# Attention row sums from the weighting exponentials, one-term maxima, and normalisation on another engine

## The chip, the cores and the metric

The kernel runs on one core of one Trainium2 chip. The metric is device microseconds of one launch. The median of three runs of the kernel before is 1118.05 us (1117.07 to 1121.98). The profile is of one more execution, which took 1115.44 us.

## The reference

The input x is 4 x 1024 x 512 in float32. Three layers follow one another, each on a layer-normed x, each added to x:

```
x = x + 0.5 * ffn(layernorm(x))        # ternary weights 512x512, plus bias
x = x + attn(layernorm(x))
x = x + 0.5 * ffn(layernorm(x))

attn: kqv = x @ Wqkv + bqkv            # 16 heads of 32
      scores = k . q / sqrt(32), masked to a triangle
      attn = softmax(scores, axis=2); out = attn^T-weighted v; out @ Wo + bo
```

## The kernel before

**Tiles and stages.** A batch has 1024 rows, 8 tiles of 128. The 16 heads are taken in 4 groups of 4; the four heads of a group lie in four bands of 32 partitions. Queries are taken in two chunks of 512 columns (c = 0, 1), keys in blocks of 128. A *step* is one key block of one chunk, or two narrow ones. Chunk 0 has 3 steps, chunk 1 has 7, so a group has 10 steps (`STEPS`), and 4 batches of 4 groups have 160.

**Precision.** Most products are made of three terms: each operand is split into a high part (`HI`, ScalarE writes it from PSUM) and a low part (`LO`, VectorE subtracts), and HI·HI, LO·HI and HI·LO are summed. The fp32 product of `values` is one of full width.

**The order of work** is written out by hand in tables of rows, one row per step (`GROUP0_ROWS` and so on). All five engines walk the same list `SLOTS`. In a slot TensorE does the scores of step n (`scores`, L1266, then the row of maxima by `mneg`, L1274), the weighting by `values` of step n−1 (L1294), and then the slot's *uses*: `A` (product for the maxima, L1232), `M`, `N` (transposes of maxima and inverses, L1242, L1247), `C` (spreading of the inverses over the heads, L1251), `T1` to `T3` (transposes of normalised tiles `hn`, L1184), `P` (queries and keys), `V` (values), `O` (output product; all L1173) and `F1`, `F2` (feed-forward, L1195). `A` runs about nine steps ahead of the scores that use its maxima.

**Softmax.** For each `A` VectorE adds the mask and takes the maximum of each row (`maximum`, L909), and writes the masked scores out. ScalarE takes exponentials of these with the accumulator on (`block_sums`, L1073), only to get the row sums. The sums of two key chunks are combined (`combine`) and inverted on VectorE (`inverse`, L937), turned into rows by `N`, sent by SP to `rall`, and spread by `C`. The exponentials that weight the values are a second set, on the turned scores (`exponentials`, L1099); GpSimd sets those above the diagonal to zero (L808), and `values` waits for that. At the end of a chunk ScalarE takes the sum out of PSUM (`evacuate`, L1063) and VectorE multiplies by the inverse (`scaled`, L945).

**The rest.** VectorE takes the statistics of a tile (L859, L861), GpSimd makes `rstd` of them (L756, L759), VectorE writes `hn` (`normal`, L878), GpSimd adds the bias (L769) and the low part of `o` (L776). PSUM has 8 banks: one collects `values`, seven go round in the order of use (`Banks`), four at once for a step's scores and for an `A`. `prob` has two buffers of four heads by 512.

## Time and profile before

| | before |
|---|---|
| median of three runs | 1118.05 us |
| the profiled execution | 1115.44 us |
| its span, first to last instruction | 1113.7 us |
| TensorE busy | 1067.9 us, 96% |
| weight loads of TensorE | 691.1 us, 62% |
| VectorE busy | 738.9 us, 66% |
| ScalarE busy | 921.7 us, 83% |
| GpSimd busy | 344.0 us, 31% |
| mean granted TensorE clock | 0.983 of full |
| DMA, mean | 70 GB/s |

An engine's busy time is the union of its instructions, and a matmul's record is longer than its pitch, since matmuls are pipelined. For what an instruction costs TensorE, the pieces of the chain are better.

### The profile page before, as it was taken

The page shows a single profiled execution, that of the slowest core. Times are in us where ns is not written, and L with a number is a line of the kernel's source. Part 1 is how long each engine was busy: PE and PEld are TensorE (multiplying, and loading weights), DVE is VectorE, ACT ScalarE, POOL GpSimd, SP SyncE. Part 2 cuts the span into 40 slices and gives each one's busy share as a digit, 9 for nine tenths or more (in the row PEclk, how much of TensorE's full clock was granted, in tenths as well). Part 3 has the DMA queues.
Part 4 walks back from the last instruction along what each step waited for, and adds up shares of the span by engine and source line. Part 5 has one row for each costly group of instructions (what it writes and reads, how often), then busy time and mean ns, then how long its engine had stood idle before and what let it go on. Part 6 is the DMA issues. An engine that isn't in the chain of part 4 may idle for free.

```text
span 1113.7 us, 26124 instructions
## 1 busy us (share of the span) xinstructions
PE 1067.9 (96%) x9472; PEld 691.1 (62%) x9472; DVE 738.9 (66%) x2306; ACT 921.7 (83%) x2577; POOL 344.0 (31%) x471
## 2 busy tenths in 40 slices
PE   5799999999999999999999999999999999999896
PEld 3576656565666565665666666675666666665465
DVE  6866577787535767789644766789744667765344
ACT  2269998999989989889988988878988998999641
POOL 3841232233001313345201322435401322311343
PEclk8898999999999999999999999999999999998999
DMA  6463211021004110421112211421112212000121
GB/s 207 153 217 125 97 50 40 3 78 50 24 19 154 32 59 31 158 73 43 38 41 87 77 59 50 144 78 40 51 40 86 69 40 69 21 12 13 60 66 38
DMA packets 42015, 77.71 MB, mean 70 GB/s; under 512 B 5536, under 2 KB 11680, under 8 KB 41888
## 3 DMA queue, kind: packets, MB, share of 16 engines
q1 hardware_dynamic: 41888, 76.04, 20.5%
q8 instruction: 76, 1.25, 0.5%
q14 instruction: 51, 0.42, 0.1%
HBM read 49.81 MB, written 25.17 MB: 67 GB/s over the span
## 4 chain that ended last, share of the span: by engine, by line
PE 76%; ACT 11%; DVE 6%; issue 2%; POOL 2%; DMA 1%; SPq 0%; DVEq 0%; ACTq 0%; POOLq 0%
PE bank L1173 31%; PE bank L1294 10%; PE bank L1232 10%; PE bank L1266 10%; PE bank L1195 7%; ACT masked_scores L1073 6%; ACT prob L1099 4%; PE bank L1184 3%; PE bank L1274 3%; DVE masked_scores L909 2%; DVE st L859 1%; DMA xt<-in_L_attn_x_dram 1%; DVE hn L878 1%; POOL xt L769 1%; PE bank L1251 1%
## 5 line engine op out<-in xcount | busy, mean ns | idle before, releaser
L909 DVE CUSTOM_DVE_ANT_0 masked_scores<-bank,mask 128x512 f32<-128x512 f32 (+3 forms) x768 | 379.6, 554 | 221.3 <-PE bank L1232 220.2
L1073 ACT ACTIVATE masked_scores<-masked_scores,mst 128x512 f32<-128x512 f32 (+3 forms) x768 | 467.7, 620 | 2.9 <-DVE mst L909 2.9
L1099 ACT ACTIVATE prob<-bank 128x512 f32<-128x512 f32 (+1 forms) x640 | 302.0, 559 | 58.5 <-PE bank L1274 57.4
L1173 PE MATMUL bank<-hT,wqk 128*128 128x512 f32 x768 | 190.9, 397 | 0.0
L808 POOL TENSOR_SCALAR_AFFINE_SELECT prob<-prob 128x512 f32<-128x512 f32 (+1 forms) x96 | 78.6, 819 | 346.5 <-ACT prob L1099 345.8
L1266 PE MATMUL bank<-qT,kT 32*128 32x512 f32 (+2 forms) x2304 | 169.6, 378 | 4.5 <-DVE kT L886 1.6
L1232 PEld LDWEIGHTS bank<-kT,qT 32*128 32x128 f32 x2304 | 94.4, 185 | 115.6 <-issue 52.8
L1232 PE MATMUL bank<-kT,qT 32*128 32x512 f32 (+2 forms) x2304 | 161.2, 377 | 3.4 <-ACT prob L1099 2.6
L1173 PEld LDWEIGHTS bank<-hT,wqk 128*128 128x128 f32 x768 | 140.4, 188 | 37.9 <-ACT prob L1099 8.2
L1073 ACT ACTIVATION_READ_ACCUMULATOR masked_scores<-masked_scores,mst 128x1 f32 x768 | 156.4, 204 | 0.0
L1266 PEld LDWEIGHTS bank<-qT,kT 32*128 32x128 f32 x2304 | 97.7, 185 | 70.4 <-issue 48.4
L1195 PE MATMUL bank<-wfT,hts 128*128 128x512 f32 x512 | 138.3, 414 | 1.5 <-DVE hts L884 1.5
L1294 PE MATMUL bank<-prob,v 128*32 128x512 f32 (+3 forms) x1344 | 138.7, 500 | 0.0
L1195 PEld LDWEIGHTS bank<-wfT,hts 128*128 128x128 f32 x512 | 94.4, 194 | 24.5 <-ACT prob L1099 2.6
L769 POOL TENSOR_TENSOR xt<-xt,hb 128x512 f32<-128x512 f32 x64 | 82.3, 1286 | 77.0 <-DVE hn L878 77.0
L1173 PE MATMUL bank<-wvo,hts 128*128 128x512 f32 x384 | 97.2, 403 | 5.0 <-POOL hts L776 5.0
L1173 PE MATMUL bank<-wvo,hT 128*128 128x512 f32 x384 | 96.1, 402 | 1.2 <-DVE qT L886 1.2
L1173 PEld LDWEIGHTS bank<-wvo,hts 128*128 128x128 f32 x384 | 70.7, 190 | 24.4 <-ACT prob L1099 6.0
L1173 PEld LDWEIGHTS bank<-wvo,hT 128*128 128x128 f32 x384 | 71.3, 191 | 19.5 <-ACT prob L1099 2.7
L1184 PE MATMUL bank<-ident,hn 128*128 128x128 f32 x384 | 59.7, 284 | 13.5 <-DVE hn L878 13.5
L1274 PE MATMUL bank<-mneg,onesr 2*128 2x512 f32 (+2 forms) x768 | 69.9, 350 | 2.1 <-DMA mneg<-mrow 2.1
L859 DVE BATCH_NORM_STATS2 st<-xt 128x6 f32<-128x512 f32 x96 | 65.9, 686 | 5.2 <-DMA xt<-in_L_attn_x_dram 3.2
(87 smaller groups left out, 971.7 us busy)
## 6 DMA issues: line engine op xcount, KB each, us to landing
wqk<-weight_scratch SPq DMA_DIRECT2D x30, 512.0 KB, 3.4
wvo<-weight_scratch SPq DMA_DIRECT2D x20, 512.0 KB, 6.0
xt<-in_L_attn_x_dram SPq DMA_DIRECT2D x32, 256.0 KB, 4.2
residual_scratch<-xt SPq DMA_DIRECT2D x32, 256.0 KB, 2.0
xt<-residual_scratch SPq DMA_DIRECT2D x32, 256.0 KB, 3.1
out_dram<-xt SPq DMA_DIRECT2D x32, 256.0 KB, 2.0
o<-in_L_attn_Wqkv_dram SPq DMA_DIRECT2D x12, 256.0 KB, 4.7
weight_scratch<-o SPq DMA_DIRECT2D x6, 512.0 KB, 3.0
```

Source lines behind the costliest of these rows:

```text
L769: nc.gpsimd.tensor_tensor(to, to, (bo2 if l == 1 else hb)[:, :], ALU.add).then_inc(xb_done[l], 1)
L808: nc.gpsimd.affine_select(out=part, in_=part, compare_op=ALU.is_ge, fill=0.0, base=0, pattern=[[0, 4], [0, m], [1, P]], channel_multiplier ...
L909: nc.vector.tensor_tensor_reduce(masked_scores[:, h, at:at + n], psum(u, h)[:, at:at + n], mask[:, off:off + n], -SCALE, BIG, ALU.add, ALU ...
L1073: nc.scalar.activation(of, of, ACT.Exp, bias=mst[:, c + kc, to:to + 1], scale=-1.0, accum_out=ssum[:, c + kc, to:to + 1]).then_inc(a_free, 1)
L1099: nc.scalar.activation(prob[:, at % 2, h, off:CW], psum(("S", b, n), h)[:, off:CW], ACT.Exp, scale=SCALE)\
L1173: m = nc.tensor.matmul(psum(u), left(x, k), right(y, k), start=(n == 0), stop=(n == len(terms) - 1))
L1184: m = nc.tensor.transpose(psum(u)[:, P * k:P * k + P], hn[:, TURN[u] % 2, P * k:P * k + P], ident[:, :])
L1195: m = nc.tensor.matmul(psum(u), h[:, part, k, :], wfT[:, k, :], start=(k == 0 and part == HI), stop=(k == KC - 1 and part == LO))
L1232: m = nc.tensor.matmul(psum(u, h)[:, at:at + n], query_piece(b, g, c)[row, x, P * r:P * r + P], kT[g % 2][row, y, CW * kc:CW * kc + n], st ...
L1266: nc.tensor.matmul(psum(u, h)[:, at:at + CW - off], kT[g % 2][row, x, P * kb:P * kb + P], query_piece(b, g, c)[row, y, off:CW], start=(ter ...
L1274: m = nc.tensor.matmul(psum(u, h)[:, at:at + CW - off], onesr[row, :], mneg[row, c, off:CW], start=False, stop=(kb == keys[-1]))
L1294: m = nc.tensor.matmul(accv[HD * h:HD * h + HD, off:CW], v_of(b, g, kb, h), prob[:, at % 2, h, of:of + CW - off], start=(kb == 0), stop=(k ...
```

## The change

The block exponentials of `masked_scores` are no longer made. The sums now come from the exponentials that weight the values: `prob` gets a third buffer, the first step of a chunk stays in its buffer as the running total, and the exponentials of each later step are added to it, heads 0 and 1 by VectorE, heads 2 and 3 by GpSimd (10 additions per group and engine). A new use `E` multiplies the total by a matrix of ones, which gives each head's sums on its 32 partitions. ScalarE copies them out, a DMA lays them out over all 128 partitions, VectorE inverts them there and splits the inverse into two parts, and a DMA brings it back as rows for `C`. In the last group (`direct`) there is no such trip: `over_sums` inverts and multiplies in four pieces.

`A` is made of one term instead of three. VectorE takes the maximum of blocks off the diagonal with a plain reduction; those on the diagonal keep the masking instruction. The row of maxima is one row per head instead of a high and a low one. ScalarE instead of VectorE normalises (`hn`), with three instructions. The tables of rows are new: `E` stands in a chunk's second slot and belongs to the chunk before, `N` two slots later and `C` four; in the middle batches parts of the feed-forward move from group 2 to group 1. `evacuate` is no longer bound to `C`: it follows the exponentials of the next chunk's first step.

```diff
+def direct(b, g):
+
+    return (b, g) == (B - 1, GROUPS - 1)
...
-    "C T3.3 P | A | X3.6",
-    "N M F2.3 P | A | X3.7",
-    "P | A",
-    "C O.4 | A",
-    "O.5 | A",
-    "N T3.4 O.6 | A",
-    "M F2.4 | A",
-    "T3.5 O.7 | A | X1.0",
-    "T3.6 F2.5 | A | LV X1.1",
-    "T3.7 F2.6 P | A | X1.2",
+    "T3.3 P | A | X3.6",
+    "E M F2.3 | A | X3.7",
+    "T1.0 O.4 | A",
+    "N F1.0 P | A | X1.1",
+    "E O.5 | A",
+    "C O.6 | A",
+    "N M T3.4 P | A | X1.2",
+    "F2.4 | A",
+    "T3.5 O.7 | A",
+    "C T1.1 F2.5 P | A | LV X1.3",
...
+NPROB = 3
+
+
+def homes():
+
+
+    free, at, total = [0] * NPROB, [], None
+    for n in range(B * NSTEP):
+        first = step_of(n % STEPS)[1][0] == 0
+        here = min(range(NPROB), key=lambda m: free[m])
+        assert free[here] <= n
+        if first and total is not None:
+            free[total] = n + 2
+        if first:
+            total = here
+        free[here] = B * NSTEP + NPROB if first else n + 2
+        at.append(here)
+    return at
+
+
+HOME = homes()
...
+        def additions(n, heads):
+
+            c, keys = step_of(n % STEPS)
+            for j, kb in enumerate(keys):
+                off = first_query(c, kb)
+                yield (prob[:, HOME[chunk_first(n)], heads, off:CW],
+                       prob[:, HOME[n], heads, off - HALF * j:CW - HALF * j])
...
-                sp.wait_ge(ring_free, freed(u))
-                for part in (HI, LO):
-                    sp.dma_start(mneg[part:P:HD, c, :].bitcast(F32), mrow[:, c, part, :].bitcast(F32))\
-                        .then_inc(mrow_in[c], 16)
+                sp.wait_ge(row_done, ROWS[u] + 1)
+                sp.dma_start(mneg[0:P:HD, c, :].bitcast(F32), mrow[:, c, :].bitcast(F32)).then_inc(mrow_in[c], 16)
+
+            def sums_to_columns(u):
+
+                sp.wait_ge(sums_out, ended(u) + 1)
+                if ended(u):
+                    sp.wait_ge(inverse_done, 3 * ended(u) - 2)
+                sp.dma_start(scol[:, :], sums[0:P:HD, :].rearrange("h (j x) -> h j x", x=4 * QPC)).then_inc(sums_in, 16)
 
             def inverse_rows(u):
                 _, b, g, c = u
-                sp.wait_ge(ring_free, freed(u))
+                sp.wait_ge(inverse_done, 3 * ended(u) + 3)
                 if ended(u):
                     sp.wait_ge(ring_full, full(("C", b, g, c - 1) if c else ("C", *before(b, g), 1)))
                 for part in (HI, LO):
-                    sp.dma_start(rall[4 * part:4 * part + 4, :].bitcast(F32), rrow[:, part, :].bitcast(F32))\
-                        .then_inc(rall_in, 16)
+                    sp.dma_start(rall[4 * part:4 * part + 4, :].bitcast(F32).rearrange("h (j x) -> h j x", x=4 * QPC),
+                                 rsplit[:, part, :].bitcast(F32)).then_inc(rall_in, 16)
...
+            def add(n):
+
+                f = chunk_first(n)
+                if n == f:
+                    return
+                if diagonal(n % STEPS):
+                    pool.wait_ge(masked, diagonals(n))
+                else:
+                    pool.wait_ge(s_exp, 4 * n + 4)
+                pool.wait_ge(value_done, f + 1)
+                for j, (to, of) in enumerate(additions(n, slice(2, 4))):
+                    if ADDED[n - 1]:
+                        pool.wait_ge(added_pool, ADDED[n - 1] + j)
+                    nc.gpsimd.tensor_tensor(to, to, of, ALU.add).then_inc(added_pool, 1)
...
+                if s.step is not None and step(s.b, s.step):
+                    add(step(s.b, s.step) - 1)
+                elif (s.b, s.row) == (B, 0):
+                    add(B * NSTEP - 1)
...
-                    if EARLIER[u] is not None:
-                        dve.wait_ge(a_free, block_at(EARLIER[u], h))
+                    written = COUNTED[u] + max(0, h - 1) * len(u[5])
+                    if kc == c and written:
+                        dve.wait_ge(a_max, written)
                     for j, r, at, n, off in block_tiles(u):
-                        to = 4 * h + r
-                        nc.vector.tensor_tensor_reduce(masked_scores[:, h, at:at + n], psum(u, h)[:, at:at + n],
-                                                       mask[:, off:off + n], -SCALE, BIG, ALU.add, ALU.min,
-                                                       mst[:, c + kc, to:to + 1]).then_inc(a_max, 1)
+                        of, to = psum(u, h)[:, at:at + n], mst[:, c + kc, 4 * h + r:4 * h + r + 1]
+                        if kc < c:
+                            i = nc.vector.tensor_reduce(to, of, AX, ALU.max)
+                        else:
+                            i = nc.vector.tensor_tensor_reduce(masked_scores[:, h % 2, at:at + n], of, mask[:, off:off + n], 1.0, -BIG,
+                                                               ALU.add, ALU.max, to)
+                        i.then_inc(a_max, 1)
                 if u == maxima(b, g, 1)[-1]:
                     dve.wait_ge(a_max, block_at(u))
-                    nc.vector.tensor_tensor(mcol[:, :], mst[:, 1, :], mst[:, 2, :], ALU.min).then_inc(mcol_done, 1)
-                    dve.wait_ge(mcol_done, group(b, g))
-                    for n in range(2):
-                        i = nc.vector.tensor_tensor(msh[:, n, :], mst[:, 1 + n, :], mcol[:, :], ALU.subtract)
-                    i.then_inc(shift_done, 1)
-
-            def combine(u):
-
-                at = group(u[1], u[2])
-                dve.wait_ge(shift_exp, at)
-                nc.vector.tensor_tensor(msh[:, :, :], msh[:, :, :], ssum[:, 1:3, :], ALU.mult).then_inc(inverse_done, 1)
-                dve.wait_ge(inverse_done, 4 * at - 2)
-                nc.vector.tensor_tensor(msh[:, 0, :], msh[:, 0, :], msh[:, 1, :], ALU.add).then_inc(inverse_done, 1)
+                    nc.vector.tensor_tensor(mcol[:, :], mst[:, 1, :], mst[:, 2, :], ALU.max).then_inc(mcol_done, 1)
+
+            def add(n):
+
+                f = chunk_first(n)
+                if n == f:
+                    return
+                if diagonal(n % STEPS):
+                    dve.wait_ge(masked, diagonals(n))
+                else:
+                    dve.wait_ge(s_exp, 4 * n + 2)
+                dve.wait_ge(value_done, f + 1)
+                for j, (to, of) in enumerate(additions(n, slice(0, 2))):
+                    if ADDED[n - 1]:
+                        dve.wait_ge(added, ADDED[n - 1] + j)
+                    nc.vector.tensor_tensor(to, to, of, ALU.add).then_inc(added, 1)
...
+                at = 3 * ended(u)
+                dve.wait_ge(sums_in, 16 * ended(u) + 16)
+                nc.vector.reciprocal(rcol[:, :], scol[:, :]).then_inc(inverse_done, 1)
+                if ended(u):
+                    dve.wait_ge(rall_in, 32 * ended(u))
+                dve.wait_ge(inverse_done, at + 1)
+                nc.vector.tensor_copy(rsplit[:, HI, :], rcol[:, :]).then_inc(inverse_done, 1)
+                dve.wait_ge(inverse_done, at + 2)
+                nc.vector.tensor_tensor(rsplit[:, LO, :], rcol[:, :], rsplit[:, HI, :].bitcast(F32), ALU.subtract)\
+                    .then_inc(inverse_done, 1)
...
+            def over_sums(u):
 
                 _, b, g, c = u
+                dve.wait_ge(ring_full, full(u))
                 dve.wait_ge(accv_free, ended(u) + 1)
-                dve.wait_ge(ring_full, full(u))
-                of = chunk(b, CHUNKS * g + c)
-                nc.vector.tensor_tensor(of, psum(u), of, ALU.mult).then_inc(ring_free, 1)
+                for r in range(QPC):
+                    at = slice(P * r, P * r + P)
+                    of = chunk(b, CHUNKS * g + c)[:, at]
+                    if c:
+                        dve.wait_ge(piece_done, r + 1)
+                    nc.vector.reciprocal(sums[:, at], psum(u)[:, at]).then_inc(inverse_done, 1)
+                    dve.wait_ge(inverse_done, 3 * ended(("E", b, g, 0)) + QPC * c + r + 1)
+                    nc.vector.tensor_tensor(of, of, sums[:, at], ALU.mult).then_inc(piece_done, 1)
...
-            def block_sums(u, heads):
-
-                _, b, g, c, kc, _ = u
-                for h in heads:
-                    for j, r, at, n, _ in block_tiles(u):
-                        to = 4 * h + r
-                        act.wait_ge(a_max, block_at(u, h, j))
-                        of = masked_scores[:, h, at:at + n]
-                        nc.scalar.activation(of, of, ACT.Exp, bias=mst[:, c + kc, to:to + 1], scale=-1.0,
-                                             accum_out=ssum[:, c + kc, to:to + 1]).then_inc(a_free, 1)
-                if u == maxima(b, g, 1)[-1] and 3 in heads:
-                    act.wait_ge(shift_done, group(b, g))
-                    nc.scalar.activation(msh[:, :, :], msh[:, :, :], ACT.Exp, scale=-1.0).then_inc(shift_exp, 1)
...
+            def sums_away(u):
+
+                act.wait_ge(ring_full, full(u))
+                if ended(u):
+                    act.wait_ge(sums_in, 16 * ended(u))
+                nc.scalar.activation(sums[:, :], psum(u), ACT.Identity).then_inc(sums_out, 1)
+
+            def normal(u):
+                kind, b, t = u
+                l = int(kind[1]) - 1
+                k = TURN[u]
+                if k >= 2:
+                    act.wait_ge(ring_full, full(TRANSPOSED[k - 2]))
+                if l == 0:
+                    act.wait_ge(*loaded(xw(kind, b, t)))
+                act.wait_ge(rs_done[l], tile(b, t))
+                nc.scalar.activation(nmean[:, l, t:t + 1], mv[:, l, t, 0:1], ACT.Identity, scale=-1.0).then_inc(shift_done, 1)
+                act.wait_ge(shift_done, 2 * k + 1)
+                nc.scalar.activation(shift[:, l, t:t + 1], nmean[:, l, t:t + 1], ACT.Identity, scale=rstd[:, l, t:t + 1])                    .then_inc(shift_done, 1)
+                act.wait_ge(shift_done, 2 * k + 2)
+                nc.scalar.activation(hn[:, k % 2, :], x_tile(xw(kind, b, t)), ACT.Identity, bias=shift[:, l, t:t + 1],
+                                     scale=rstd[:, l, t:t + 1]).then_inc(hn_done, 1)
...
+                held = [m for m in range(at) if HOME[m] == HOME[at]][-1:]
+                for m in held:
+                    if chunk_first(m) == m:
+                        i = m % STEPS
+                        act.wait_ge(ring_full, full(("E", m // NSTEP, m % NSTEP // STEPS, 1 if i else 0)))
+                    else:
+                        act.wait_ge(value_done, m + 1)
+                        act.wait_ge(added, ADDED[m])
+                        act.wait_ge(added_pool, ADDED[m])
                 for h in range(4):
-                    nc.scalar.activation(prob[:, at % 2, h, off:CW], psum(("S", b, n), h)[:, off:CW], ACT.Exp, scale=SCALE)\
+                    nc.scalar.activation(prob[:, HOME[at], h, off:CW], psum(("S", b, n), h)[:, off:CW], ACT.Exp, scale=SCALE)\
...
-                    for term, (x, y) in enumerate(((HI, HI), (LO, HI), (HI, LO))):
-                        for j, r, at, keys, _ in block_tiles(u):
-                            n = max(HALF, keys)
-                            for h in range(4):
-                                if term == 0 and j == 0:
-                                    bank_free(u, h)
-                                row = slice(HD * h, HD * h + HD)
-                                m = nc.tensor.matmul(psum(u, h)[:, at:at + n], query_piece(b, g, c)[row, x, P * r:P * r + P],
-                                                     kT[g % 2][row, y, CW * kc:CW * kc + n], start=(term == 0 and j == 0),
-                                                     stop=(term == 2 and j == len(u[5]) - 1))
+                    for j, r, at, keys, _ in block_tiles(u):
+                        n = max(HALF, keys)
+                        for h in range(4):
+                            if j == 0:
+                                bank_free(u, h)
+                            row = slice(HD * h, HD * h + HD)
+                            m = nc.tensor.matmul(psum(u, h)[:, at:at + n], query_piece(b, g, c)[row, HI, P * r:P * r + P],
+                                                 kT[g % 2][row, HI, CW * kc:CW * kc + n], start=(j == 0),
+                                                 stop=(j == len(u[5]) - 1))
...
+                elif kind == "E":
+                    n = last_step(u)
+                    pe.wait_ge(added, ADDED[n])
+                    pe.wait_ge(added_pool, ADDED[n])
+                    for h in range(4):
+                        m = nc.tensor.matmul(psum(u)[HD * h:HD * h + HD, :], ones[:, 0:HD], prob[:, HOME[chunk_first(n)], h, :],
+                                             start=True, stop=True)
+                    m.then_inc(ring_full, 1)
...
-                        row = slice(HD * h, HD * h + 2)
+                        row = slice(HD * h, HD * h + 1)
```

## Rows read from the trace of the kernel before

**Rows 1.** The page: TensorE's part of the busy line, and the chain by engine.
```profile
PE 1067.9 (96%) x9472; PEld 691.1 (62%) x9472; DVE 738.9 (66%) x2306; ACT 921.7 (83%) x2577; POOL 344.0 (31%) x471
...
PE 76%; ACT 11%; DVE 6%; issue 2%; POOL 2%; DMA 1%; SPq 0%; DVEq 0%; ACTq 0%; POOLq 0%
```

**Rows 2.** Stretches: us from:to, length, then busy us of each engine.
```profile
0.00:103.20 103.20, 80.51 (x440) 58.55 (x442) 74.66 (x183) 50.11 (x132) 52.60 (x75) 0.93 0.54 176
103.20:218.90 115.70, 112.80 (x1056) 69.10 (x1052) 77.58 (x268) 108.77 (x310) 31.41 (x46) 0.97 0.17 57
218.90:276.20 57.30, 55.49 (x549) 33.86 (x542) 44.93 (x143) 55.99 (x158) 21.35 (x24) 1.00 0.19 62
276.20:340.50 64.30, 64.30 (x586) 41.88 (x582) 29.83 (x113) 56.26 (x163) 4.91 (x6) 1.00 0.13 43
340.50:463.50 123.00, 122.97 (x1160) 79.78 (x1158) 86.22 (x276) 110.67 (x311) 38.31 (x47) 1.00 0.24 80
463.50:532.40 68.90, 67.53 (x618) 44.02 (x614) 61.28 (x179) 58.64 (x161) 32.71 (x49) 1.00 0.18 59
532.40:598.30 65.90, 65.87 (x602) 43.14 (x594) 32.48 (x119) 57.35 (x158) 7.86 (x9) 1.00 0.16 54
856.20:975.50 119.30, 119.30 (x1137) 76.58 (x1134) 82.93 (x267) 110.53 (x317) 34.94 (x50) 1.00 0.16 52
975.50:1027.40 51.90, 50.56 (x501) 29.66 (x497) 32.89 (x118) 50.35 (x146) 7.47 (x8) 0.94 0.04 13
1027.40:1113.70 86.30, 72.12 (x515) 47.30 (x507) 35.27 (x72) 35.25 (x85) 32.38 (x46) 0.94 0.16 53
```

**Rows 3.** The chain in order of time, 521 to 534: start, us it takes, what.
```profile
521.06 1.00 PE bank L1294 x8
522.05 1.15 PE bank L1232 x20
523.20 0.59 PE bank L1184 x4
523.79 1.85 PE bank L1195 x8
...
527.57 0.72 PE bank L1232 x10
...
528.89 2.75 PE bank L1173 x12
531.63 0.90 PE bank L1266 x10
532.53 0.24 PE bank L1274 x4
...
533.56 0.90 PE bank L1232 x10
```

**Rows 4.** The page's groups: busy us, mean ns of one, idle time before.
```profile
L1073 ACT ACTIVATE masked_scores<-masked_scores,mst 128x512 f32<-128x512 f32 (+3 forms) x768 | 467.7, 620 | 2.9 <-DVE mst L909 2.9
```

**Rows 5.** Groups by shape: subtractions of two inputs, VectorE and GpSimd.
```profile
L884 DVE TENSOR_TENSOR hts<-bank,hts 128x512 fp32r<-128x512 f32 x64 | 43.6, 681 | 15.5 <-ACT hts L1039 15.5
...
L776 POOL TENSOR_TENSOR hts<-o,hts 128x512 fp32r<-128x512 f32 x8 | 10.3, 1293 | 18.5 <-ACT hts L1092 18.5
...
L776 POOL TENSOR_TENSOR hts<-o,hts 128x128 fp32r<-128x128 f32 x16 | 7.5, 471 | 18.9 <-ACT hts L1092 18.9
...
L884 DVE TENSOR_TENSOR rrow<-bank,rrow 16x128 fp32r<-16x128 f32 x32 | 8.8, 274 | 3.0 <-ACT rrow L1032 3.0
```

**Rows 6.** Timeline of the tail: start, us, engine, instruction [idle before].
```profile
1087.55 1.59 POOL L776 TENSOR_TENSOR hts<-o,hts 128x384 fp32r<-128x384 f32 x2
1087.69 1.14 DVE L878 TENSOR_SCALAR hn<-xt,mv,rstd 128x512 f32<-128x512 f32 x1 [1.03 <-POOL rstd L759]
...
1091.39 0.55 DVE L878 TENSOR_SCALAR hn<-xt,mv,rstd 128x512 f32<-128x512 f32 x1 [1.02 <-POOL rstd L759]
```

**Rows 7.** Who waited for whom: us in total, times, longest.
```profile
DVE masked_scores L909 <- PE bank L1232: 220.2, 133, 6.0
```

More of the change, by code:

```diff
@@ L238 @@
     "T3.5 O.7",
[L239 to L241 removed]
+    "F2.4",
+    "T3.6 F2.5",
+    "T3.7 F2.6",
     "F2.7",
@@ L278, in __init__ @@
         self.b, self.step, self.row = b, step, row
-        self.whole, self.blocks, self.loads, weights = rows
+        whole, self.blocks, self.loads, weights = rows
+        self.whole = [u for u in whole if u[0] != "N"]
+        self.inverses = [u for u in whole if u[0] == "N"]
         self.weights = [n for _, n in weights]
     def uses(self):
-        return self.blocks + self.whole
+        sums = [u for u in self.whole if u[0] == "E"]
+        return sums + self.blocks + [u for u in self.whole if u[0] != "E"]
 def plan():
@@ L336 @@
 assert len(USES) == len(set(USES))
-SPLIT = {u: n for n, u in enumerate([u for s in SLOTS for kinds in ("M N", "T1 T2 T3", "P") for u in s.uses()
+SPLIT = {u: n for n, u in enumerate([u for s in SLOTS for kinds in ("T1 T2 T3", "P") for u in s.uses()
                                      if u[0] in kinds.split()])}
@@ L389, in use @@
                 self.full[u] = full
-            if u[0] not in ("A", "V") and u not in [TURNED[n] for n in BY_ACT]:
+            if u[0] not in ("A", "V", "M", "E") and u not in [TURNED[n] for n in BY_ACT]:
                 self.freed[u] = freed
@@ L713, in _ @@
                     load(w)
+                for u in s.inverses:
+                    inverse_rows(u)
                 for u in s.uses():
@@ L981, in _ @@
                     first_stats(k)
-                for u in s.uses():
-                    if u[0] == "N":
-                        inverse(u)
-                    elif u[0] == "C" and u[3] == 0:
-                        combine(u)
-                if s.step is None and k > 1:
-                    for u in NORMALISED[k]:
-                        normal(u)
+                for u in s.inverses:
+                    inverse(u)
                 for u in s.uses():
@@ L992, in _ @@
                         use(u)
-                if s.step is not None or k == 1:
-                    for u in NORMALISED[k]:
-                        normal(u)
+                if s.step is not None:
+                    add(step(s.b, s.step))
                 for u in s.uses():
@@ L1105, in _ @@
                     act.wait_ge(s_full, step(b, s.step) + 1)
-                    if step(b, s.step) >= 2:
-                        act.wait_ge(value_done, step(b, s.step) - 1)
                     exponentials(b, s.step)
-                if k and SLOTS[k - 1].blocks:
-                    block_sums(SLOTS[k - 1].blocks[-1], (3,))
+                    g, i = s.step // STEPS, s.step % STEPS
+                    if i == CHUNK_STEPS[0]:
+                        evacuate(b, g, 0)
+                    elif i == 0 and step(b, s.step):
+                        evacuate(*before(b, g), 1)
+                elif (b, s.row) == (B, 0):
+                    evacuate(B - 1, GROUPS - 1, 1)
                 for u in s.uses():
-                    if u[0] in ("M", "N"):
-                        high(u)
-                    elif u[0] == "C":
-                        evacuate(u)
+                    if u[0] == "M":
+                        row(u)
+                    elif u[0] == "E" and not direct(u[1], u[2]):
+                        sums_away(u)
                 for u in s.uses():
@@ L1121, in _ @@
                         high_output(u)
-                for u in s.blocks:
-                    block_sums(u, range(4) if u != s.blocks[-1] else range(3))
+                for u in NORMALISED[k]:
+                    normal(u)
                 for u in s.uses():
@@ L1146, in bank_free @@
                     pe.wait_ge(a_max, block_at(w, n))
+                elif w[0] == "M":
+                    pe.wait_ge(row_done, ROWS[w] + 1)
+                elif w[0] == "E" and direct(w[1], w[2]):
+                    pe.wait_ge(piece_done, QPC * w[3] + QPC)
+                elif w[0] == "E":
+                    pe.wait_ge(sums_out, ended(w) + 1)
                 else:
```

275 lines of the change are left out of this document (132 added, 143 removed).

## The prediction

> **What bounds the kernel now.** I began with the page. TensorE is busy 96% of the span, and the chain that ended last is 76% TensorE, 11% ScalarE and 6% VectorE [rows 1]. ScalarE's part is mostly one line, the exponentials of `masked_scores` (L1073), which exist only to get row sums. Next I cut the span into the head, 15 groups of ten steps and the last group with the tail, and read busy time by stretch [rows 2]. The reader is to see two kinds of stretch. In batch 0, groups 0 to 2 (115.7 us for two, then 57.3), ScalarE is busy 94 to 98% of the time, and TensorE's own work fills only 50 to 52 us a group. I count that work by the pitches of the chain [rows 3]: 0.90 + 0.24 us for a step's scores, 1.00 for its values, 0.90 for a use of `A`, less for narrow ones, which is 29.9 us a group with `C`, `M` and `N`; then 2.75 us for each `P`, `V` or `O`, 1.85 for each `F`, 0.59 for each `T` of the rows. From 276.2 us on the span follows TensorE: groups of 60 to 69 us, in which this count leaves 1 to 4 us open. One group of each middle batch is close on VectorE too: 61.28 us busy of 68.9. GpSimd is busy 5 to 33 us per group and mostly waits. Head and tail are latency: TensorE works 80.5 us of 103.2, and 72.1 of 86.3.
>
> **The change, part by part.** Durations are pitches of the chain where matmuls overlap [rows 3].
>
> *Maxima with one term.* Each of 160 uses of `A` issues a third of its matmuls. A use takes 0.90 us with twelve 512-wide matmuls, 1.15 with twenty-four 256-wide, 0.72 with twelve 384-wide [rows 3]. A group has six, two and two of them: 9.1 us (the last five at the tile sizes of chunk 0 and the diagonal). For four matmuls with 32 or fewer rows, the nearest row is the one that adds `mneg`: 0.24 for four 512-wide ones [rows 3]; eight 256-wide ones are as long. I take 0.24, so 2.4 us a group, and 6.7 us are saved. Between 0.20 and 0.40 a use the saving is 5.1 to 7.1.
>
> *Sums by a ones matmul (`E`), twice a group.* Four fp32 products of 128 rows by 512 columns, of the same form as a step of `values`: 1.00 us for 8 instructions [rows 3], so +2.0 a group. The transpose `N`, smaller than the `T` of 0.59, goes twice, some 0.15 each by its share of columns; `C` and `M` stay. Net for TensorE: −6.7 + 2.0 − 0.3 = −5.0, and as the pieces beside it do not all compress I take −4.7 us a group, 75 us in all.
>
> *ScalarE loses the block exponentials:* 467.7 us [rows 4], and the reads of the accumulator behind them. It gains 96 normalisations: two instructions on 128x1 and one on 128x512, about 1.1 us with the waits on itself, 106 us; 30 copies of sums at 0.6. It lands near 600 us, about 38 us a group. So it bounds no group, and groups 0 to 2 of batch 0 and group 2 of batch 3 are freed to the next limit. Its normalisation waits on GpSimd's `rstd`, and the high parts of `P` and the next step's exponentials are queued behind it. I cost that at nothing, because most rows leave a step or more (5 to 6 us) between statistics and use. If GpSimd runs a step late, it costs 1 to 2 us a row.
>
> *VectorE.* It loses `hn` (96 at 0.5 to 0.55 [rows 6], about 48 us), the low parts of `M` and `N` and the shifts (2 us a group), and gets about 1.2 us of inverses. The off-diagonal maxima become a plain reduction, which I cost as equal, 0.69 us. It gains the additions. There is no addition of this size in the trace. From its own 16x128 and 128x512 subtractions, 274 and 681 ns [rows 5], a column costs 1.06 ns above 138 ns: 1.22, 0.95, 0.68 and 0.41 us for two heads of 512, 384, 256 and 128 columns. A group has 4, 2, 2 and 2 of them: 9.0 us. Net +8.1 − 0.5 for each `hn`: from 77.6 for groups 0 and 1 of batch 0 to about 43 + 48 us, from 44.9 to 48 in group 2, and about 61 in the dense group (61.28 now; it loses 13 `hn` and two tiles move to the group before).
>
> *GpSimd.* Its rows give 471 ns for 128 columns and 1293 for 512 [rows 5], 2.14 ns a column: 2.39, 1.84, 1.29 and 0.74 us, 17.3 us a group, 277 in all. It would be busy 22 to 50 us a group, about 620 us in total. The masking select is queued behind the addition of the step before, and `values` waits for it. But it has about 4 us of room: exponentials end 3.3 us into a step and `values` comes a step and 1.1 us later. Hidden.
>
> *Do the two kinds of addition disturb each other?* This decides the sum. The trace shows one such case: `hn` (SBUF to SBUF) takes 0.55 us by itself and 1.14 when GpSimd's subtraction of two SBUF tiles is running, ending just behind it [rows 6]. Operations of VectorE with one input in PSUM keep their time beside GpSimd. The additions have both inputs in SBUF, and no row shows that form beside GpSimd. Bounds: zero per addition (they pass each other), and a whole GpSimd addition, 1.7 us on average (17.3 / 10), every time. I take half the collisions: GpSimd will be busy about 65% of a group, a hit leaves half an operation, about 0.9 us, so 5.5 us a group. I choose this nearer to the disturbed row because source and destination are alike.
>
> The Trainium skill ("SBUF — State Buffer", section "Who interferes with whom") says that a VectorE instruction with two SBUF inputs contends with a GpSimd instruction that reads SBUF, and that the second to issue blocks until the first has ended. No row here has that form; the rows of `hn` agree with the blocking as such. By that rule the loss is never zero, and the sum is the forecast or the slow rival below, not the fast one.
>
> *New waits.* `E` waits for both engines' additions of the chunk's last step; scores of the next step are queued behind it on TensorE. It stands a step and a half behind them, so nothing. Exponentials wait for the additions of two steps before: nothing unless VectorE is over a step late. On SP the column DMA of the sums waits for ScalarE's copy, with x loads, stores and `mneg` rows queued behind; one `mneg` DMA less and 1 to 2 us of waiting, hidden by a step or more. VectorE's inverse waits for that DMA two steps later, with the maxima queued behind: nothing expected, up to 1 us a time.
>
> **The sum**, against the profiled execution: 1113.7 us of span and 1.7 us around it. A group is the later of TensorE's work and VectorE's with its losses, and 2 us on top where both are near. Head 103.2 → 101 (its last 25 us wait on block exponentials, but weights and loads remain). Batch 0: the first two groups 115.7 together → 51.5 + 55, then 57.3, 64.3 → 55.5, 60. Middle batches: the first two groups 123.0 together → 57 + 60, then 68.9, 65.9 → 67, 63.5, all twice. Batch 3: the first two 119.3 together → 55.5 + 58, then 51.9 → 47 [rows 2]. Last group and tail 86.3 → 85: the sums now come after the last exponentials, and `over_sums` puts a reciprocal between, which eats most of the gain. Total 101 + 222 + 495 + 160.5 + 85 = 1063.5, and with 1.7 us outside, 1065. The median of the runs is 0.2% above the profiled run. I forecast 1064.
>
> **The rivals.**
> *No disturbance, TensorE stays the only bound.* Additions pass or fall where the other engine idles. For it: GpSimd has room, and VectorE waits 220.2 us for the maxima's matmuls [rows 7]. Against it: both additions are released by the same event, and VectorE is near 48 of 50 us even so. Taking the 5.5 us out: batch 0 50, 50, 51, 60; middle 56, 59, 64, 63.5; batch 3 54.5, 57, 44; 1037 in all; with a smaller tail and fewer gaps, 1015.
> *VectorE takes the place of TensorE, slower than now.* Each VectorE addition waits out a whole GpSimd addition, because GpSimd starts at the end of the exponentials or of the mask, about 3.3 to 4.4 us into a step, and VectorE only behind the maxima, about 5 us in. Place: every step but the first of a chunk. Price: 17.3 us a group instead of 5.5. Groups are then 62 to 81 us long, as 48 + 17 + 2 in batch 0 and 61 + 17 + 3 in the dense group: 1150 to 1200 us. It decides from 1.0 us of loss per addition on: each us a group costs about 12 us in all, so 10 us a group gives 1118.
> *The gain is mostly given back.* The same at 0.8 to 0.95 us, or the chains behind GpSimd and the DMA of the sums show as gaps of 2 to 3 us a group: 1085 to 1112.
> That TensorE's work does not fall can hardly be: two thirds of the matmuls of a use go.
>
> **How the numbers follow.** Forecast (1045 to 1085) 0.47; no disturbance (1010 to 1045) 0.28; gain mostly given back 0.14; no net change 0.04; slower 0.07. The range runs from 1015 to 1105. A measurement of this kernel can tell about 0.5% from no change. Faster by more than that: 0.47 + 0.28 + 0.12 = 0.87; within it 0.05; slower 0.08.
>
> **What the profile after would show.** L1232's successor takes a quarter of a us per use and a third of its count. No `masked_scores` on ScalarE, and its share near 57%. `E` at 1.0 us without idle before it. VectorE near 78% and GpSimd near 58% busy. The disturbance would show as a mean of the VectorE additions of 128x1024 well above 1.2 us, or of GpSimd's above 2.4. If it is small, these means stand and the groups of batch 0 come to 50 us. It would prove me wrong if TensorE idled before `E` or before the transposes, which is the path over GpSimd and ScalarE that I cost at nothing, or if plain reductions differ from 0.69 us: 256 of them at 0.1 us are 26 us of VectorE.

## The result and the profile after

| | before | after |
|---|---|---|
| median of the runs | 1118.18 us (4 runs) | 1146.78 us (4 runs, 1143.29 to 1150.02) |
| profiled execution, span | 1115.44, 1113.7 us | 1150.02, 1148.3 us |
| mean granted clock | 0.983 | 0.958 |

The ratio is 1.025, with a 95% interval of 1.021 to 1.029. The change makes the kernel 2.5% slower. I had forecast 1064 us, and a range up to 1105.

The page of the kernel after: busy times, granted clock in 40 slices (tenths), and the chain by engine.

```profile
PE 1070.7 (93%) x8158; PEld 663.4 (58%) x8158; DVE 900.0 (78%) x2058; ACT 608.8 (53%) x1311; POOL 661.4 (58%) x631
...
PEclk8899989797999999989999999999999999998989
...
PE 58%; DVE 21%; POOL 12%; issue 6%; ACT 2%; DMA 1%; SPq 0%; POOLq 0%; DVEq 0%; ACTq 0%
```

ScalarE fell from 921.7 to 608.8 us as expected. But 1536 fewer matmuls of `A` left TensorE's busy time where it was, 1070.7 us, and the chain now runs over VectorE and GpSimd for a third of the span, where it was 8% [rows 1]. The clock is low in more slices.

Stretches of the kernel after, cut at the same steps as in [rows 2]; us from:to, length, busy us of TensorE, weight loads, VectorE, ScalarE, GpSimd, then granted clock, DMA share and GB/s.

```profile
0.00:97.70 97.70, 76.17 (x352) 55.03 (x354) 63.12 (x150) 46.20 (x97) 50.40 (x75) 0.93 0.57 186
97.70:219.20 121.50, 116.09 (x884) 66.84 (x880) 97.36 (x239) 61.70 (x128) 71.32 (x66) 0.89 0.17 54
219.20:285.10 65.90, 61.17 (x467) 34.93 (x461) 56.13 (x124) 41.35 (x91) 41.69 (x35) 0.87 0.17 54
285.10:347.20 62.10, 62.06 (x508) 39.05 (x500) 41.46 (x103) 29.43 (x66) 22.67 (x16) 1.00 0.14 41
347.20:476.20 129.00, 124.11 (x1000) 77.00 (x992) 110.45 (x251) 68.22 (x143) 79.69 (x71) 0.99 0.23 74
476.20:548.80 72.60, 67.05 (x524) 42.15 (x516) 65.16 (x146) 45.28 (x98) 49.99 (x50) 0.95 0.18 59
...
1003.50:1053.40 49.90, 47.68 (x423) 25.89 (x418) 40.88 (x106) 27.12 (x58) 25.66 (x18) 0.95 0.05 13
1053.40:1148.30 94.90, 75.76 (x527) 47.34 (x519) 51.88 (x83) 40.90 (x93) 54.58 (x58) 0.91 0.14 48
```

Against [rows 2]: the head is 5.5 us shorter. Groups 0 and 1 of batch 0 are 121.5 us (115.7 before, 106.5 forecast), group 2 65.9 (57.3, 55.5), the first two of batch 1 129.0 (123.0, 117), the dense group 72.6 (68.9, 67). The last group with the tail lost 8.6 us. The head, the fourth group of batch 0 (62.1 against 64.3) and the third of batch 3 (49.9 against 51.9) gained; the others lost, and no single one explains the result. VectorE is busy 80 to 90% of the groups that lost most, and never all of one.

The additions of the kernel after, by shape: busy us, mean ns of one.

```profile
L852 POOL TENSOR_TENSOR prob<-prob 128x1024 f32<-128x1024 f32 x64 | 174.1, 2720 | 56.0 <-ACT prob L1207 55.3 <-POOL prob L852 0.3
...
L1010 DVE TENSOR_TENSOR prob<-prob 128x1024 f32<-128x1024 f32 x64 | 114.0, 1781 | 1.4 <-POOL prob L895 1.4
...
L1010 DVE TENSOR_TENSOR prob<-prob 128x256 f32<-128x256 f32 x32 | 34.0, 1061 | 1.1
```

I had costed them at 1.22 us, 0.41 us (VectorE) and 2.39 us (GpSimd) by themselves, and 5.5 us a group of blocking on VectorE. All of VectorE's take 224.4 us where 16 groups of 9.0 make 144: 5.0 us a group of blocking. GpSimd's are held up too, by 39 us in all, which I had at nothing. So VectorE's term was sized well; its price was not. The timeline of one step shows how it is paid: start, us, instruction, and idle time before it with what ended it.

```profile
708.78 2.38 POOL L852 TENSOR_TENSOR prob<-prob 128x1024 f32<-128x1024 f32 x1
708.85 3.40 DVE L1010 TENSOR_TENSOR prob<-prob 128x1024 f32<-128x1024 f32 x1
...
711.47 0.50 PE L1348 MATMUL bank<-kT,qT 32*128 32x512 f32 x2
712.17 0.68 DVE L972 TENSOR_TENSOR xt<-bank,xt 128x512 f32<-128x512 f32 x1
...
712.91 0.49 PE L1348 MATMUL bank<-kT,qT 32*128 32x512 f32 x2 [0.94 <-DVE xt L972]
```

GpSimd's addition starts 0.07 us earlier. VectorE's ends 1.1 us behind the end of GpSimd's: 3.40 us for an instruction of 1.22. Behind it in VectorE's queue stands the residual of the last output product, which frees a PSUM bank. `A` of the next slot needs four banks of the ring of seven and gets two: its second pair of matmuls starts 1.44 us after the first, 0.94 us of it idle.

GpSimd's bias instruction (L837, also of two SBUF inputs) blocks in the same way, and VectorE blocks GpSimd:

```profile
126.18 1.29 POOL L837 TENSOR_TENSOR xt<-xt,hb 128x512 f32<-128x512 f32 x1 [1.66 <-ACT hn L1177]
...
126.99 1.57 DVE L1010 TENSOR_TENSOR prob<-prob 128x1024 f32<-128x1024 f32 x1
127.43 3.35 POOL L852 TENSOR_TENSOR prob<-prob 128x1024 f32<-128x1024 f32 x1
```

VectorE's addition ends 1.08 us behind the bias, and GpSimd's then ends 2.2 us behind VectorE's. Over the whole trace, 109 of VectorE's 160 additions lose time in this way, 0.74 us each: 49 us behind GpSimd's additions and 32 us behind its bias and low-part instructions.

### The profile page after: what moved, and what is told of

Same layout as the page of the kernel before. It is cut to its first block, busy times and chain, and to the rows that moved or that the text cites. A ratio compares the mean times of both kernels' runs of the same rounds, so it can differ in the third digit from the quotient of the medians.

```text
span 1148.3 us, 22475 instructions
## 1 busy us (share of the span) xinstructions
PE 1070.7 (93%) x8158; PEld 663.4 (58%) x8158; DVE 900.0 (78%) x2058; ACT 608.8 (53%) x1311; POOL 661.4 (58%) x631
## 3 DMA queue, kind: packets, MB, share of 16 engines
q8 instruction: 66, 1.08, 0.4%
## 4 chain that ended last, share of the span: by engine, by line
PE 58%; DVE 21%; POOL 12%; issue 6%; ACT 2%; DMA 1%; SPq 0%; POOLq 0%; DVEq 0%; ACTq 0%
PE bank L1290 26%; PE bank L1414 8%; PE bank L1386 7%; DVE prob L1010 6%; POOL prob L852 5%; DVE mst L988 5%; PE bank L1348 5%; PE bank L1312 5%; POOL xt L837 3%; PE bank L1369 2%; PE bank L1301 2%; PE bank L1394 2%; DVE st L946 2%; POOL prob L895 2%; DVE masked_scores L990 1%
## 5 line engine op out<-in xcount | busy, mean ns | idle before, releaser
L852 POOL TENSOR_TENSOR prob<-prob 128x1024 f32<-128x1024 f32 (+3 forms) x160 | 315.4, 1971 | 61.6 <-ACT prob L1207 55.3
L990 DVE CUSTOM_DVE_ANT_0 masked_scores<-bank,mask 128x128 f32<-128x128 f32 (+3 forms) x512 | 218.1, 487 | 75.6 <-PE bank L1348 75.5
L1010 DVE TENSOR_TENSOR prob<-prob 128x1024 f32<-128x1024 f32 (+3 forms) x160 | 224.4, 1403 | 16.5 <-POOL prob L895 15.1
L1290 PE MATMUL bank<-hT,wqk 128*128 128x512 f32 x768 | 198.1, 408 | 0.1
L988 DVE TENSOR_REDUCE mst<-bank 128x1 f32<-128x512 f32 x256 | 158.6, 682 | 49.2 <-PE bank L1348 49.1
L1348 PEld LDWEIGHTS bank<-kT,qT 32*128 32x128 f32 x768 | 47.4, 188 | 151.0 <-issue 94.3
L1348 PE MATMUL bank<-kT,qT 32*128 32x512 f32 (+2 forms) x768 | 109.7, 444 | 26.0 <-DVE xt L975 16.7
L837 POOL TENSOR_TENSOR xt<-xt,hb 128x512 f32<-128x512 f32 x64 | 90.9, 1421 | 33.6 <-ACT hn L1177 31.8
L824 POOL TENSOR_SCALAR ve<-mv 128x1 f32<-128x1 f32 x96 | 18.3, 190 | 131.5 <-DVE mv L948 127.1
L1177 ACT ACTIVATE hn<-xt,shift,rstd 128x512 f32<-128x512 f32 x96 | 78.3, 815 | 3.2
```

Source lines behind the costliest of these rows:

```text
L837: nc.gpsimd.tensor_tensor(to, to, (bo2 if l == 1 else hb)[:, :], ALU.add).then_inc(xb_done[l], 1)
L852: nc.gpsimd.tensor_tensor(to, to, of, ALU.add).then_inc(added_pool, 1)
L988: i = nc.vector.tensor_reduce(to, of, AX, ALU.max)
L990: i = nc.vector.tensor_tensor_reduce(masked_scores[:, h % 2, at:at + n], of, mask[:, off:off + n], 1.0, -BIG, ALU.add, ALU.max, to)
L1010: nc.vector.tensor_tensor(to, to, of, ALU.add).then_inc(added, 1)
L1290: m = nc.tensor.matmul(psum(u), left(x, k), right(y, k), start=(n == 0), stop=(n == len(terms) - 1))
```

## The experiments

All are edits of the changed kernel but one. The theory under test: the additions, by the time they take on VectorE with the blocking included, hold up the release of PSUM banks and so TensorE. Where additions are left out, the sums are not those of a whole chunk, and only the time is of use.

**Without any addition.** All calls of both `add` functions go, with the waits on them.

```diff
-                if s.step is not None:
-                    add(step(s.b, s.step))
...
-                    pe.wait_ge(added, ADDED[n])
-                    pe.wait_ge(added_pool, ADDED[n])
```

> The changed kernel with all 320 additions left out (the sums are then those of a chunk's first step), all else kept. Theory: the additions, by their time on VectorE and GpSimd and by blocking each other, are what turned the expected gain into a loss; without them TensorE is the bound and the time is 1035 to 1060 us, with the clock low for at most 50 us. Rival: the loss comes from elsewhere (E at 1.0 us, the trip of the sums, normalisation on ScalarE, the short A); then the time stays above 1100 us.

Measured: 1063.4 us (two runs, 1057.3 and 1069.4), 3 us above the theory's range and far below the rival. The additions cost 83 us (77 to 89 by these two runs); what is left of the change gives 54 us, where the prediction's case without disturbance (1037 us, at best 1015), additions included, had 80 to 100. The chain of this run in order of time (start, us, what) shows why:

```profile
714.99 0.86 PE bank L1359 x8
...
730.11 0.97 PE bank L1376 x11
731.09 0.23 PE bank L1384 x3
731.32 0.99 PE bank L1404 x8
732.31 0.43 PE bank L1340 x2
732.74 0.59 PE bank L1293 x4
```

L1340 is `A` with one term. It takes 0.43 us, although nothing waits here, and not the 0.24 us of the `mneg` rows (L1384 here) that I took from [rows 3]. 160 uses at 0.2 us more are 32 us. (From one matmul's start to the next, `A` takes 70.6 us in this whole trace, 0.44 a use.) `E` (L1359) takes 0.86 us, a little less than my 1.00.

**VectorE's additions alone, GpSimd's alone.** The other engine's calls and the waits on them are left out.

```diff
-                if s.step is not None and step(s.b, s.step):
-                    add(step(s.b, s.step) - 1)
-                elif (s.b, s.row) == (B, 0):
-                    add(B * NSTEP - 1)
```

> GpSimd's 160 additions left out, VectorE's kept where they are. Theory of contention: VectorE's additions fall from a mean of 1403 ns to about 950, as the width alone gives (1.22, 0.95, 0.68, 0.41 us), and the time falls to 1060 to 1085 us. Rival, VectorE's own load and the place of its additions: they keep VectorE late by the same amount, and the time stays at 1115 us or more.

> VectorE's 160 additions left out, GpSimd's kept. Theory that VectorE is what is late (its additions stand in front of the instructions that free PSUM banks): 1045 to 1070 us, nearly as without any. Rival, GpSimd's queue is what is late (mask and rstd behind additions of 2 to 3 us): the time stays above 1100 us.

Measured: 1096.8 us with VectorE's alone, 33 us above none; 1076.9 with GpSimd's alone, 14 above none. The first lies between theory and rival, the second 7 us above the theory's range and far from its rival. Together they should cost 47 us and cost 83. Either more load than VectorE can hide or the meeting of the two makes the missing 36 us; the next run separates these. By shape, first VectorE's alone, then GpSimd's alone:

```profile
L1006 DVE TENSOR_TENSOR prob<-prob 128x1024 f32<-128x1024 f32 x64 | 91.1, 1423 | 0.0
...
L1006 DVE TENSOR_TENSOR prob<-prob 128x256 f32<-128x256 f32 x32 | 17.0, 532 | 1.1
```

```profile
L852 POOL TENSOR_TENSOR prob<-prob 128x1024 f32<-128x1024 f32 x64 | 152.9, 2388 | 56.7 <-ACT prob L1204 55.9 <-POOL prob L852 0.3
```

GpSimd's are within 0.1% of my estimate. VectorE's of 1024 columns are 0.2 us above theirs on average, and all 160 have a mean of 1.07 us, not the 0.95 expected: they meet GpSimd's bias and low-part instructions, which remain and cost them 28 us in this run.

**One SBUF input instead of two on VectorE.** GpSimd's additions stay, and VectorE reads as many elements as an addition has columns, but has no second input, and writes two columns and not the total.

```diff
-                    nc.vector.tensor_tensor(to, to, of, ALU.add).then_inc(added, 1)
+                    nc.vector.tensor_reduce(rsum[:, :], of, AX, ALU.add).then_inc(added, 1)
```

> The changed kernel in which each of VectorE's 160 additions is a sum over the same new exponentials into two scalars (one SBUF input instead of two, about the same length; the totals of heads 0 and 1 are then left out). GpSimd's additions stay. Theory of contention: operations with one SBUF input do not block and are not blocked by GpSimd's; VectorE's take 1.2 us at 1024 columns without spread, GpSimd's go back to 2388 ns from 2720, the time falls from 1147 to about 1105 us, the two halves' costs simply added (33 + 14 us above 1063). Rival, load: the same load on both engines gives the same loss; 1135 us or more.

Measured: 1089.6 us, lower than even the theory's 1105, and 57 us below the changed kernel, with the same count of instructions in the same places. By shape:

```profile
L853 POOL TENSOR_TENSOR prob<-prob 128x1024 f32<-128x1024 f32 x64 | 152.8, 2388 | 56.7 <-ACT prob L1208 55.9 <-POOL prob L853 0.3
...
L1011 DVE TENSOR_REDUCE rsum<-prob 128x2 f32<-128x1024 f32 x64 | 77.4, 1210 | 1.4 <-POOL prob L896 1.4
```

Both engines are back at their undisturbed times. VectorE is busy 815.8 us in this run, 900.0 with the additions: the 84 us of blocking on it, and 39 us on GpSimd (315.4 against 276), turn into 57 us of the span. The form of the operands does it, not the load. That agrees with the Trainium skill ("SBUF — State Buffer", section "Who interferes with whom"): two SBUF inputs contend with GpSimd's reads, a reduction does not. The wide write that the edit also drops is not enough by itself: in the changed kernel the residual additions (L975, one input in PSUM, 512 columns written to SBUF) take 741 ns beside GpSimd's two-input instructions and 744 away from them.

**The addition last in its slot.** VectorE takes the slot's products out of PSUM first.

```diff
-                if s.step is not None:
-                    add(step(s.b, s.step))
                 for u in s.uses():
                     if u in PRODUCTS:
                         use(u)
+                if s.step is not None:
+                    add(step(s.b, s.step))
```

> The whole changed kernel, with VectorE's addition moved behind the instructions of the same slot that take products out of PSUM (P, V, F, O), ahead of the statistics. Theory of place: TensorE's waits at A for banks held by these products (about 50 us in the changed kernel) mostly go, the clock falls less often, and the time is 1100 to 1125 us. Rival: the load of VectorE is what counts and the order does not; within 1% of the changed kernel, 1135 to 1158 us.

Measured: 1133.6 us, 1.1% better than the changed kernel, slower than the theory's 1100 to 1125 and than the kernel before (ratio 1.014, 1.010 to 1.017), and 1.4 us off the rival's range. The place matters a little. Summed from one matmul's start to the next over the whole trace, `A` falls from 119.5 to 73.5 us, near the 70.6 without additions, and the scores with their `mneg` rows rise from 215.9 to 243.5: over half of the wait moves on to the next user of banks. I read this as VectorE being late, whichever release stands last.

**Three terms of `A` put back.**

```diff
-                    for j, r, at, keys, _ in block_tiles(u):
+                    for term, (x, y) in enumerate(((HI, HI), (LO, HI), (HI, LO))):
+                        for j, r, at, keys, _ in block_tiles(u):
```

> The changed kernel with the three terms of A put back. Theory: a good part of what the one-term A saves turns into waits for PSUM banks at A and at the scores, because VectorE sets the pace; the three terms cost only 0 to 30 us more than 1147. Rival, TensorE is the bound: 160 uses at 0.45 to 0.6 us more, 70 to 95 us, 1215 to 1240 us.

Measured: 1183.3 us, 36 us above the changed kernel, between both: my 0 to 30 was a little low. By pitches, 0.90 against 0.43 us, the two terms are worth some 75 us, and only half of that shows. Waits in the changed kernel hide a part. Another part may be clock: its mean is 0.979 here against 0.958, which is 25 us of full clock withheld against 48. No run tells the two apart.

**Other splits of the additions:** one head to VectorE and three to GpSimd, all four to VectorE, all four to GpSimd. The edit of the first:

```diff
-                for j, (to, of) in enumerate(additions(n, slice(0, 2))):
+                for j, (to, of) in enumerate(additions(n, slice(0, 1))):
...
-                for j, (to, of) in enumerate(additions(n, slice(2, 4))):
+                for j, (to, of) in enumerate(additions(n, slice(1, 4))):
```

> The changed kernel with the additions split one head to VectorE and three to GpSimd. GpSimd alone with two heads cost only 14 us, VectorE alone 33. Theory that VectorE's load and place are what costs: its additions are half as long, the time falls to 1110 to 1130 us. Rival, GpSimd: with 0.19 + 2.14 ns a column a step's addition takes 3.5 us, 25 us a group, and blocks VectorE longer each time; 1140 us or more.

> All four heads' additions on VectorE, none on GpSimd; everything else as changed. VectorE then has 266 us of additions (138 ns and 1.06 ns a column, 16.6 us a group) where it now spends 224 with the blocking. Theory that the blocking of the two engines is the larger part: with more addition time on VectorE but hardly any blocking (GpSimd's bias and low-part instructions remain) the time is no higher than 1147, 1115 to 1150 us. Rival, VectorE's time as such sets the pace, whatever fills it: 42 us more of it cost 40 us or more, 1185 us or above.

> All four heads' additions on GpSimd, none on VectorE. GpSimd then has 0.19 us and 2.14 ns a column, 4.6 us for a step of 512, 33 us a group and 525 us in all, which with its 339 us makes 80% of the span. Theory that GpSimd's queue has room as long as VectorE does not contend: 1090 to 1125 us, below 1147. Rival: the mask select and rstd behind 4.6 us additions make TensorE wait at values and at the transposes; 1150 us or more.

Measured: 1184.6, 1169.8 and 1160.2 us. My theory failed all three times. The rival held with one to three (1140 or more) and with all on GpSimd (1150 or more); all on VectorE lies between, 20 us above my range and 15 below the rival. One to three is the worst, where I expected 1110 to 1130. By shape, in that run:

```profile
L852 POOL TENSOR_TENSOR prob<-prob 128x1536 f32<-128x1536 f32 x64 | 232.2, 3628 | 44.1 <-ACT prob L1207 43.3 <-POOL prob L852 0.3
...
L1010 DVE TENSOR_TENSOR prob<-prob 128x512 f32<-128x512 f32 x64 | 112.0, 1750 | 5.8 <-POOL prob L895 5.8
```

An addition of half the size takes VectorE 1.75 us, as long as one of two heads, since it waits out the longer one of GpSimd (0.68 us by itself). With all on VectorE the blocking on it falls to some 28 us (294 us of additions where I had costed 266), but its busy time is 960.7 us, 60 above the changed kernel's. With all on GpSimd, VectorE is busy only 732.7 us; the mask comes late, and TensorE waits for it. Who waited for whom in that run (us in total, times, longest):

```profile
ACT nmean L1171 <- POOL rstd L827: 61.3, 25, 5.1
...
PE bank L1410 <- POOL prob L895: 38.7, 21, 4.0
```

**One-term `A` alone, in the kernel before.** The edit of the change to `A` and nothing else.

> The kernel before with the one-term A alone. If the pitch of a short A is 0.24 us as forecast, TensorE loses 5 to 6.7 us of work a group; in the groups bounded by ScalarE (batch 0 and group 2 of batch 3) nothing comes of it, since ScalarE stays at 55 to 58 us a group and becomes the bound in the others too: 1060 to 1085 us. Rival: the short A is no shorter than 0.45 us with its weight loads, and it waits for banks; then 1090 to 1118 us.

Measured: 1088.2 us, a ratio of 0.975 (0.971 to 0.979) to the kernel before, between the two expectations and nearer to the rival, which had the pitch right. ScalarE's share of the chain is 20% in this run. This part of the change is worth 28 us by itself, and it is the best complete version of this study, 59 us faster than the whole change.

## Why the prediction was wrong

**The cost of the additions by themselves was right** (1.21, 0.95, 0.68 and 0.42 us are the lowest of VectorE's, and 2388, 1840, 1290 and 739 ns are GpSimd's means without VectorE's). **VectorE's blocking was right in kind and size**, 5.0 us a group against 5.5: 68% of the additions are hit, where I took 65%, at 0.74 us each, where I took 0.9. I also named the deciding point: 10 us a group was to give 1118. Half of that gave more.

**The step that failed is "A group is the later of TensorE's work and VectorE's with its losses, and 2 us on top where both are near."** In groups 0 and 1 of batch 0 VectorE is busy 97.4 us, less than the 102 of the forecast (43 + 48, and 11 of losses), and the stretch lasts 121.5, not 106.5. The forecast gave the blocking 27 us of time (1037 to 1064); in the runs the additions with their blocking cost 83, and 57 of these go when VectorE has one input. VectorE does its work in a fixed order, with four PSUM banks for `A` and four for the scores out of seven. The reading that fits the timeline of the step: TensorE waits whenever one release comes late, and does not get the time back. Sorted by VectorE's busy time, seven runs make one row:

| VectorE busy, us | time, us | mean clock | what |
|---|---|---|---|
| 686 | 1063 | 0.974 | no additions |
| 694 | 1077 | 0.984 | GpSimd's alone |
| 816 | 1090 | 0.981 | one input |
| 840 | 1097 | 0.979 | VectorE's alone |
| 884 | 1134 | 0.962 | addition last |
| 900 | 1147 | 0.958 | the change |
| 961 | 1170 | 0.953 | all on VectorE |

From 686 to 840 us, where VectorE is 77% busy, 154 us cost 34; the next 60 us cost 50, and 60 more cost 23. Off the row are the run with three terms, which gives TensorE more work, and the two in which GpSimd is the fullest, 64 and 74% busy (one to three, and all on GpSimd). In the changed kernel both engines are under 80%, and still TensorE does not hide them: that is what the forecast lacked. The table is an ordering by one number, not a proof that only this number counts: a VectorE that is blocked counts as busy, and the clock falls along the same row.

**The pitch of a short `A` was mis-sized.** 0.24 us from the `mneg` rows, which load one or two rows of weights, against 0.43 measured; 32 us in all. My upper bound of 0.40 missed too. It accounts for the run without additions standing at 1063 and not near 1030. From start to start, `A` takes 153.1 us before, 70.6 in the changed kernel without additions and 119.5 with them: 49 of the 83 us saved are given back.

**The clock was not in the sum.** A mean of 0.958 over 1148.3 us is 48 us of full clock withheld, 0.983 over 1113.7 is 19: up to 29 us of the difference. The stretch before, at and after one fall:

```profile
100.00:140.90 40.90, 38.15 (x293) 22.46 (x292) 28.05 (x68) 20.94 (x44) 20.03 (x17) 0.96 0.31 105
140.90:151.10 10.20, 10.20 (x53) 4.85 (x53) 9.86 (x23) 4.82 (x10) 9.85 (x9) 0.50 0.14 53
...
160.00:198.90 38.90, 36.33 (x298) 21.05 (x290) 33.36 (x85) 21.99 (x47) 19.71 (x24) 1.00 0.10 29
```

A granted 0.50 is the lower level, 1.2 GHz. Just before it TensorE had waited for VectorE's maxima:

```profile
136.41 0.50 PE L1386 MATMUL bank<-qT,kT 32*128 32x512 f32 x1
138.69 2.15 PE L1386 MATMUL bank<-qT,kT 32*128 32x512 f32 x11 [1.78 <-DVE mst L988]
```

With one input on VectorE the clock is 0.981 over 1086.2 us, 21 us withheld. So about 27 of the 57 us that the blocking costs may be clock, a second price of the same waits. How much of this the waits would have cost at full clock stays open; no run holds the waits and frees the clock. Repeated runs of one kernel do not settle it: without additions they took 1057.3 us at a clock of 0.988 and 1069.4 at 0.974, but with one-term `A` alone 1086.8 at 0.986 and 1089.0 at 0.973.

**Point by point.** ScalarE near 57%: 53%. VectorE near 78%, GpSimd 58%: 78 and 58%, which is luck. My own terms give VectorE 820 us without the blocking and 908 with it, 77 and 85% of 1064, and GpSimd 621; measured are 900.0 and 661.4, in a longer span. `E` without a wait before it: 1.9 us of waits in all, right. The transposes wait 12.4 us for `hn` from ScalarE, where it was 13.5 for VectorE: by these waits the moved normalisation costs TensorE nothing, as forecast; no run moves it back. GpSimd's additions were to be hidden; by themselves they cost 14 us. The inverses wait for no DMA to speak of. The plain reduction takes 682 ns against 687: right. The tail was to gain 1.3 us and lost 8.6; its clock is 0.91, and the reciprocals of `over_sums` take 951 ns each for 128 columns. The slow rival named the right mechanism and the right place, but with a whole GpSimd addition lost each time, at a chance of 7%. Its 1150 us came near the measured time by a loss over three times too large (17.3 us a group against 5.0), priced too low. The sign depended on this rate of exchange, which I took as known. A slip besides: 1065 was of the profiled execution, and the 0.2% that I name would have made the forecast 1067.

## What to carry to other kernels

When elementwise work of two SBUF inputs is split between VectorE and GpSimd, do not add their times as if they ran side by side: the one that starts later waits out the other's instruction and then takes nearly its full time. A smaller share for VectorE only makes it wait out a longer one. Not splitting was no way out here: all on VectorE and all on GpSimd were slower still. When an engine frees the buffers of the bounding engine, its time has a price before it looks full: here 0.2 us for each us up to 77% busy, and 0.4 to 0.8 from there on, the clock included. A shortened product must be costed by a row of its own shape of weights.

## What the runs showed of the hardware

- VectorE's addition of 128x1024 in float32, both inputs in SBUF, takes 1.21 us alone and up to 3.47 beside GpSimd's; a reduction over the same elements stays at 1.21 beside it.
- In all 44 cases in which such an addition was held up in the changed kernel, it ended 1.08 us (1076 to 1088 ns) behind the GpSimd instruction that was running, an addition, the bias or a low part. GpSimd's of 128x1024, started during VectorE's, ended 2.22 to 2.24 us behind it, in 22 cases. Only a small part of either (0.1 to 0.2 us) overlaps the wait.
- GpSimd is held up as well: 2388 ns on average without VectorE's additions, 2720 with them. One of 128x2048 takes 4585 without them.
- Four products of 32 rows by 512 columns in four bands, with weights of 32x128, take 0.43 us where four with one row of weights take 0.24.
- TensorE's clock was at the lower level for some 96 us (by the mean of 0.958) in a kernel in which TensorE is 93% busy, against some 38 (by 0.983) in one at 96%.
